# A longer clear between layer one's result scatters, and more results scattered before layer two's second sort

## The chip, the cores and the metric

One NeuronCore of a Trainium2 chip. The metric is the device time of one execution in microseconds, in float32 throughout. The profile names the engines PE (TensorE matmul; PEld its weight load), DVE (VectorE), ACT (ScalarE), POOL (GpSimd) and SP (SyncE, which issues most DMAs). POOL issues the indirect ones.

## The reference

The input x is 4 batches of 1024 tokens, width 128. Three sublayers follow one another, each a residual: a mixture of experts, an attention, the same mixture of experts again.

```python
x = x + 0.5 * ffn(layernorm(x))      # layer one
x = x + attn(layernorm(x))           # linear attention, 16 heads of 8, chunks of 128
x = x + 0.5 * ffn(layernorm(x))      # layer two, same weights

# ffn: each token goes to one of 8 experts (128 -> 512 -> 128)
expert_idx = argmax(xf @ Wr.T + br)
h = relu(xf @ W1[e].T + b1[e]);  y = h @ W2[e].T + b2[e]     # e = expert_idx of the token
```

## The kernel before, in words

**Sorting by expert.** Tokens lie in SBUF in 32 tiles of 128 rows. An expert layer works on tiles whose 128 tokens all have the same expert, so the rows are first sorted: for each token tile DVE computes where its rows go (`slot_of`, L792), and POOL writes the rows to DRAM with one indirect DMA per tile (`sort_rows`, L375 to L387). The sorted tiles are called slots here. A layer is sorted in two units, so that the first can be worked on while the second is still being routed. Layer one's units have 12 and 20 token tiles (19 and 27 slots), layer two's 16 and 16 (23 and 23 slots): 46 slots in each layer, 92 in all, numbered G = 0 to 91.

**One slot.** SP loads the slot's 128 rows of 576 bytes into a ring of 24 (`load_slot`, L309) and its expert's first weights, 256 KB, into a ring of four (`load_w1`, L318). DVE normalises (L818) and adds the second bias (L826), PE transposes (L1053), ACT copies (L509), PE multiplies up (L1061, 8 matmuls), ACT (L524) and DVE (L833) apply bias and relu, PE multiplies down (L1071, 8 matmuls), and DVE adds the result to the row in the ring (`add_y`, L840), which raises `y_done`. In the text "result n" is the n-th L840, of slot G = n - 1. Engines are tied by semaphores: PE signals the transpose, each half of up, and down to ACT, DVE and SP.

**Scatter.** POOL waits for `y_done`, clears a scratch tile that nothing reads (`pause`, L368, the MEMSET of L372) and sends the 128 rows back to their tokens' places with an indirect DMA (`scatter`, L389 to L399), to x1 in layer one and to the output in layer two. So a clear does nothing but put time between two indirect DMAs.

```python
for G in range(first, end):
    pool.wait_ge(y_done, G + 1)
    if G >= SCATTER_SEMS:
        wait_scattered(pool, G - SCATTER_SEMS)
    pause(256)
    pool.indirect_dma_start(...)
```

**Order on POOL** (L468 to L479), written by hand and kept in order by the engine:

```python
sort_rows(0); sort_rows(1)                  # sort_rows(1) has pause(512) before each DMA
scatter(0, LAYER_TILES - LATE)              # G = 0..37
for b in range(BATCH): outer_part(0, 1, b)
scatter(LAYER_TILES - LATE, LAYER_TILES - 6)  # G = 38, 39
for n in range(STEPS): attention(n)         # turn 0 holds G = 40..45, one by one
sort_rows(2)
scatter(LAYER_TILES, LAYER_TILES + EARLY_SCATTERS)
sort_rows(3)
scatter(LAYER_TILES + EARLY_SCATTERS, LAYERS * LAYER_TILES)
```

`sort_rows(0)`, `(2)` and `(3)` have no clear between their DMAs. Layer two's second sort, `sort_rows(3)`, waits for `slot_of` of that unit, which DVE computes beside slots 11 to 14 of the layer (the hooks of L1003 and L1004).

**Order on SP.** `loads` (L331) issues, in loop step G, the slot load of G + 6 and then the weight load of G + 3. The weight load waits until PE is done with slot G - 1's up product. The first slot load of a unit (G = 69 for the last one) waits for all of that unit's sort DMAs, and everything behind it on SP waits too, the weight load of G = 66 first. After all of layer one's scatters SP loads x1 back (L349), in attention's turn 0, for the layer norms of turn 1.

Of the kernel before, what the change touches and what calls it, by code (L numbers as in the profile page):

```python
# [83 lines left out]
def wait(eng, sem, value):  # L84
    if value > 0:
        eng.wait_ge(sem, value)
# [15 lines left out]
def build(nc, x, w1t, bias, w2t, wrt, br, wqkv, wg1t, wg2, wo, gamma, beta, decay, const, out):  # L102
    with ExitStack() as ctx:
# [147 lines left out]

        helped = lambda n, h: n < STEPS - 1 and h % 2 == 0
        ln_turn = lambda k: max(k + 1, 0)
        EARLY_SCATTERS = 6
        LATE = 8
        ROUTE_TURN = SPLIT[1][0] - 1 + 3

# [7 lines left out]
        layer_of = lambda G: G // LAYER_TILES  # L265
# [93 lines left out]
        def _(pool):  # L359
# [8 lines left out]
            def pause(columns):  # L368

                k = pauses[0]  # L370
                wait(pool, paused, k - 1)
                pool.memset(scratch[k % 2][:, 0:columns], 0.0).then_inc(paused, 1)  # L372
                pauses[0] += 1

            def sort_rows(u):  # L375
                unit = UNIT[u]
                pool.wait_ge(rows_kept, unit.layer * STEPS + (unit.first + unit.tiles) // BATCH)
                pool.wait_ge(fill_ready, 4)
                pool.wait_ge(ids_ready, 1 + 2 * min(u + 1, GROUPS))
                pool.wait_ge(slots_known[u], 1)  # L380
                pool.wait_ge(slots_filled[u], 16)
                for t in range(unit.tiles):
                    if u == 1:
                        pause(512)
                    pool.indirect_dma_start(  # L385
                        slots_in[u], bass.IndirectOffsetOnAxis(ap=slot_of[u][:, t:t + 1], axis=0),
                        row_of(unit.first + t), None).then_inc(rows_sorted[u], 16)  # L387

            def scatter(first, end):  # L389

                for G in range(first, end):
                    pool.wait_ge(y_done, G + 1)
                    if G >= SCATTER_SEMS:
                        wait_scattered(pool, G - SCATTER_SEMS)
                    pause(256)
                    pool.indirect_dma_start(  # L396
                        x1 if layer_of(G) == 0 else out, bass.IndirectOffsetOnAxis(ap=ids_in_ring(G), axis=0),
                        in_ring(G, 0, D), None, bounds_check=NO_TOKEN - 1,
                        oob_is_err=False).then_inc(scattered[G % SCATTER_SEMS], 16)  # L399
# [36 lines left out]
            def attention(n):  # L436

                late = lambda i: scatter(LAYER_TILES - 6 + i, LAYER_TILES - 5 + i) if n == 0 else None
                if n > 0:
                    outer_part(n, 1, 0)  # L440
# [27 lines left out]
            sort_rows(0)  # L468
            sort_rows(1)
            scatter(0, LAYER_TILES - LATE)  # L470
            for b in range(BATCH):
                outer_part(0, 1, b)
            scatter(LAYER_TILES - LATE, LAYER_TILES - 6)
            for n in range(STEPS):
                attention(n)
# [5 lines that stand above are left out]
# [821 lines left out]
```

## Time and profile before

| what | us |
|---|---|
| three runs before | 501.15, 503.57, 504.87 |
| their median | 503.57 |
| the profiled execution, whole | 504.27 |
| its span, first to last instruction | 502.5 |
| PE busy in the span | 376.0 |
| DVE busy | 347.6 |
| POOL busy | 301.8 |
| ACT busy | 192.8 |

The profile page shows shares over the whole span. Here the parts matter more: layer one's expert pass lies at about 46 to 170 us of the span, attention at 170 to 355, layer two's expert pass at 350 to 497. "remote" or "another core or an unknown queue" in a row is a wait that no event in the profile explains at the time when it ends. "issue" is idle time for which nothing was waited for that the profile shows.

### The profile page before, as it was taken

The page shows a single profiled execution, that of the slowest core. Times are in us where ns is not written, and L with a number is a line of the kernel's source. Part 1 is how long each engine was busy: PE and PEld are TensorE (multiplying, and loading weights), DVE is VectorE, ACT ScalarE, POOL GpSimd, SP SyncE. Part 2 cuts the span into 40 slices and gives each one's busy share as a digit, 9 for nine tenths or more (in the row PEclk, how much of TensorE's full clock was granted, in tenths as well). Part 3 has the DMA queues.
Part 4 walks back from the last instruction along what each step waited for, and adds up shares of the span by engine and source line. Part 5 has one row for each costly group of instructions (what it writes and reads, how often), then busy time and mean ns, then how long its engine had stood idle before and what let it go on. Part 6 is the DMA issues. An engine that isn't in the chain of part 4 may idle for free.

```text
span 502.5 us, 10537 instructions
## 1 busy us (share of the span) xinstructions
PE 376.0 (75%) x2474; PEld 331.9 (66%) x2474; DVE 347.6 (69%) x1064; ACT 192.8 (38%) x590; POOL 301.8 (60%) x386
## 2 busy tenths in 40 slices
PE   5693796699999859586797988372899720699983
PEld 2592796599988746465676776262798610699983
DVE  4937473178876796999989879994776700377861
ACT  1360452145546322336355352401565200255541
POOL 1047988856651796877847676765050378466564
PEclk9555798589999997999988979695699965699998
DMA  8982774257681008500000000012544321266630
GB/s 246 283 310 81 219 222 149 80 149 206 200 250 53 16 12 231 146 0 0 2 1 1 1 2 0 0 48 65 167 144 139 118 80 49 83 188 195 203 122 6
DMA packets 54218, 56.08 MB, mean 112 GB/s; under 512 B 6828, under 2 KB 39881, under 8 KB 53904
## 3 DMA queue, kind: packets, MB, share of 16 engines
q1 hardware_dynamic: 48736, 45.85, 31.8%
q0 software_dynamic: 4992, 8.94, 5.0%
q10 hardware_dynamic: 432, 0.63, 0.4%
q8 instruction: 23, 0.38, 0.3%
q14 instruction: 35, 0.29, 0.2%
HBM read 39.69 MB, written 17.53 MB: 114 GB/s over the span
## 4 chain that ended last, share of the span: by engine, by line
PE 26%; issue 25%; DVE 19%; POOL 15%; SPq 5%; another core or an unknown queue 4%; DMA 1%; ACT 1%; DVEq 1%; POOLq 1%; ACTq 0%
PE bank L1061 9%; PE bank L1071 9%; POOL out_x L396 7%; POOL scratch L372 3%; POOL slots_in L385 3%; DVE o_in L879 3%; PE bank L1153 2%; DVE st L666 2%; DVE qS L870 2%; PE bank L1119 2%; SPq L288 1%; PE bank L1025 1%; SPq L298 1%; POOL x L396 1%
## 5 line engine op out<-in xcount | busy, mean ns | idle before, releaser
L1061 PE MATMUL bank<-slot_xT,w_ring 128*128 128x128 f32 x736 | 110.0, 293 | 19.0 <-issue 8.6
L1061 PEld LDWEIGHTS bank<-slot_xT,w_ring 128*128 128x128 f32 x736 | 98.7, 206 | 23.8 <-issue 18.1
L385 POOL DMA_INDIRECT slots_in<-rows,slot_of x64 | 62.0, 969 | 67.1 <-DVE slot_of L792 51.3
L833 DVE TENSOR_SCALAR hT_b<-bank,b_cur 128x128 f32<-128x128 f32 x184 | 55.7, 344 | 40.3 <-remote 24.9
L1071 PE MATMUL bank<-w_sb,hT_a 128*128 x368 | 62.0, 293 | 23.1 <-issue 18.4
L1119 PE MATMUL bank<-outer_all,decay_sb 128*128 128x256 f32 x256 | 71.2, 405 | 10.4 <-POOL outer_all L277 6.8
L277 POOL TENSOR_TENSOR outer_all<-qkv 128x512 f32<-128x512 f32 x60 | 63.3, 1084 | 12.6 <-ACT qkv L562 12.5
L524 ACT ACTIVATE hT_a<-bank,b_cur 128x128 f32<-128x128 f32 x184 | 57.5, 364 | 31.5 <-remote 15.3
L1071 PEld LDWEIGHTS bank<-w_sb,hT_a 128*128 128x128 f32 x368 | 50.8, 200 | 27.7 <-issue 27.5
L1119 PEld LDWEIGHTS bank<-outer_all,decay_sb 128*128 128x128 f32 x256 | 49.4, 203 | 27.7 <-issue 8.1
L372 POOL MEMSET scratch<- 128x256 f32 (+1 forms) x112 | 40.3, 360 | 42.7 <-DVE ring L840 33.6
L840 DVE SCALAR_TENSOR_TENSOR ring<-bank,ring 128x128 f32<-128x128 f32 x92 | 26.6, 289 | 47.4 <-remote 21.0
L1071 PE MATMUL bank<-w_sb,hT_b 128*128 x368 | 58.5, 283 | 0.0
L396 POOL DMA_INDIRECT out_x<-ring x46 | 44.8, 974 | 19.0 <-POOL scratch L372 14.4
L879 DVE TENSOR_REDUCE o_in<-qS 128x64 f32<-128x256 f32 (+1 forms) x64 | 53.6, 858 | 0.0
L396 POOL DMA_INDIRECT x<-ring x46 | 45.4, 986 | 13.5 <-POOL scratch L372 10.5
L870 DVE TENSOR_TENSOR qS<-bank,qkv 128x512 f32<-128x512 f32 x64 | 43.3, 679 | 12.2 <-PE bank L1119 8.7
L1071 PEld LDWEIGHTS bank<-w_sb,hT_b 128*128 128x128 f32 x368 | 50.9, 200 | 0.0
L517 ACT ACTIVATE b_cur<-b_t 128x4 f32 x92 | 18.9, 205 | 69.9 <-DVE hT_b L833 48.3
L818 DVE TENSOR_SCALAR slot_n<-ring 128x128 f32<-128x128 f32 x92 | 44.0, 479 | 0.8 <-DMA ring<-slots_in 0.6
L434 POOL TENSOR_TENSOR qS<-qS 128x256 f32<-128x256 f32 x28 | 20.4, 729 | 39.3 <-DVE qS L870 39.2
L509 ACT ACTIVATE slot_xT<-bank 128x128 f32<-128x128 f32 x92 | 25.1, 273 | 46.8 <-remote 35.2
(119 smaller groups left out, 562.3 us busy)
## 6 DMA issues: line engine op xcount, KB each, us to landing
w_ring<-in_w1t SPq DMA_DIRECT2D x92, 256.0 KB
ring<-slots_in SPq DMA_DIRECT2D x92, 72.0 KB
slots_in<-fill SPq DMA_DIRECT2D x2, 1656.0 KB, 13.0
rows<-in_x SPq DMA_DIRECT2D x8, 256.0 KB, 6.2
w_sb<-in_w2t SPq DMA_DIRECT2D x1, 2048.0 KB
rows<-x SPq DMA_DIRECT2D x8, 256.0 KB, 4.9
slots_in<-fill SPq DMA_DIRECT2D x1, 1944.0 KB, 15.1
slots_in<-fill SPq DMA_DIRECT2D x1, 1368.0 KB, 8.7
```

The lines of the kernel that those rows point to most:

```text
L277: return eng.tensor_tensor(u_.rearrange("p (h d e) -> p h d e", d=HD, e=HD), k_.rearrange("p (h d) e -> p h d e", d=HD), v_, ALU.mult)
L372: pool.memset(scratch[k % 2][:, 0:columns], 0.0).then_inc(paused, 1)
L385: pool.indirect_dma_start(slots_in[u], bass.IndirectOffsetOnAxis(ap=slot_of[u][:, t:t + 1], axis=0), row_of(unit.first + t), None).then_in ...
L396: pool.indirect_dma_start(x1 if layer_of(G) == 0 else out, bass.IndirectOffsetOnAxis(ap=ids_in_ring(G), axis=0), in_ring(G, 0, D), None, b ...
L524: last = nc.scalar.activation(hT_a[G % 2][:, f * P:(f + 1) * P], bank_a[:, f * P:(f + 1) * P], ACT.Relu, bias=b1_cur[G % 2][:, f:f + 1])
L818: nc.vector.tensor_scalar(slot_n[G % 3][:, :], in_ring(G, 0, D), in_ring(G, SCALE_AT, SCALE_AT + 1), in_ring(G, SHIFT_AT, SHIFT_AT + 1), A ...
L833: last = nc.vector.tensor_scalar(hT_b[G % 2][:, f * P:(f + 1) * P], bank_b[:, f * P:(f + 1) * P], b1_cur[G % 2][:, 2 + f:3 + f], 0.0, ALU. ...
L870: nc.vector.tensor_tensor(qS[h % 4][:, :].rearrange("p (b a e) -> p b a e", b=BATCH, e=HD), bank[h % 3][:, :].rearrange("p (b a e) -> p b ...
L879: nc.vector.tensor_reduce(o_in[:, h * w:(h + 1) * w].rearrange("p (a e) -> p a e", e=HD), qS[h % 4][:, :].rearrange("p (a d e) -> p a e d" ...
L1061: last = mm(to[:, f * P:(f + 1) * P], w1_ring[G % W1_BUFS][:, (2 * half + f) * P:(2 * half + f + 1) * P], slot_xT[G % 2][:, :], start=True ...
L1071: last = mm(y_bank[:, 0:D], h[:, f % 2 * P:(f % 2 + 1) * P], w2_sb[:, bass.ds(expert[G] + f * D, D)], start=(f == 0), stop=(f == FB - 1))
L1119: last = mm(to, decay_sb[:, (2 * h + a) * P:(2 * h + a + 1) * P], u, start=True, stop=True)
```

## The change

Between layer one's scatters POOL clears 128 x 512 elements, before 128 x 256. Layer two's stay at 256. And `EARLY_SCATTERS` is 15, before 6: POOL scatters G = 46 to 60 before `sort_rows(3)`, before it was G = 46 to 51.

```diff
--- before.py
+++ after.py
@@ -251,7 +251,7 @@
 
         helped = lambda n, h: n < STEPS - 1 and h % 2 == 0
         ln_turn = lambda k: max(k + 1, 0)
-        EARLY_SCATTERS = 6
+        EARLY_SCATTERS = 15
         LATE = 8
         ROUTE_TURN = SPLIT[1][0] - 1 + 3
 
@@ -392,7 +392,7 @@
                     pool.wait_ge(y_done, G + 1)
                     if G >= SCATTER_SEMS:
                         wait_scattered(pool, G - SCATTER_SEMS)
-                    pause(256)
+                    pause(512 if layer_of(G) == 0 else 256)
                     pool.indirect_dma_start(
                         x1 if layer_of(G) == 0 else out, bass.IndirectOffsetOnAxis(ap=ids_in_ring(G), axis=0),
                         in_ring(G, 0, D), None, bounds_check=NO_TOKEN - 1,
```

## Rows read from the trace of the kernel before

**Rows 1.** the page's part 4, the chain that ended last, by engine
```profile
PE 26%; issue 25%; DVE 19%; POOL 15%; SPq 5%; another core or an unknown queue 4%; DMA 1%; ACT 1%; DVEq 1%; POOLq 1%; ACTq 0%
```

**Rows 2.** windows: stretch, length, busy us by engine, PEclk, DMA share, GB/s
```profile
46.00:79.00 33.00, 27.89 (x238) 26.69 (x238) 20.62 (x70) 13.94 (x53) 29.70 (x40) 0.83 0.70 208
...
79.00:101.00 22.00, 13.50 (x64) 11.45 (x64) 5.22 (x18) 3.59 (x14) 18.40 (x29) 0.63 0.31 95
...
397.00:417.00 20.00, 6.81 (x38) 5.45 (x38) 4.24 (x18) 2.20 (x9) 15.42 (x16) 0.72 0.27 88
...
417.00:430.00 13.00, 1.81 (x8) 1.78 (x8) 0.84 (x3) 0.00 (x0) 11.52 (x19) 0.50 0.14 46
```

**Rows 3.** timeline of POOL, layer one: start us, length us, what, idle before
```profile
77.55 0.54 POOL L372 MEMSET scratch<- 128x512 f32 x1
...
79.22 0.33 POOL L372 MEMSET scratch<- 128x256 f32 x1
...
98.74 0.97 POOL L396 DMA_INDIRECT x<-ring  x1 [0.16 <-issue]
...
161.56 2.09 POOL L277 TENSOR_TENSOR outer_all<-qkv 128x512 f32<-128x512 f32 x2 [11.42 <-ACT qkv L562]
```

**Rows 4.** timeline of DVE, layer one: results 2, 11, 17 and 36
```profile
60.43 0.29 DVE L840 SCALAR_TENSOR_TENSOR ring<-bank,ring 128x128 f32<-128x128 f32 x1 [0.25 <-PE bank L1071]
...
78.03 0.29 DVE L840 SCALAR_TENSOR_TENSOR ring<-bank,ring 128x128 f32<-128x128 f32 x1
...
106.66 0.29 DVE L840 SCALAR_TENSOR_TENSOR ring<-bank,ring 128x128 f32<-128x128 f32 x1 [0.28 <-PE bank L1071]
...
142.93 0.28 DVE L840 SCALAR_TENSOR_TENSOR ring<-bank,ring 128x128 f32<-128x128 f32 x1
```

**Rows 5.** timeline of all engines behind the very first sort
```profile
48.20 0.48 PE L1053 MATMUL bank<-const_sb,slot_n 128*128 128x128 f32 x1 [0.23 <-issue]
...
52.99 0.28 ACT L509 ACTIVATE slot_xT<-bank 128x128 f32<-128x128 f32 x1 [8.29 <-remote]
```

**Rows 6.** line L818 in 46 to 79 and in 104 to 143: ns min/median/max
```profile
L818 DVE TENSOR_SCALAR slot_n<-ring x15: 335/375/803, 47.8 to 78.2; 128x128 f32<-128x128 f32 x15
...
L818 DVE TENSOR_SCALAR slot_n<-ring x20: 535/535/656, 104.4 to 141.2; 128x128 f32<-128x128 f32 x20
```

**Rows 7.** timeline of attention's turn 0, last scatter and what follows
```profile
187.45 1.02 POOL L396 DMA_INDIRECT x<-ring  x1 [0.17 <-issue]
...
189.67 2.59 SPq L327 DMA_DIRECT2D rows<-x  x5
```

**Rows 8.** timeline of POOL around the last sort
```profile
397.00 0.96 POOL L385 DMA_INDIRECT slots_in<-rows,slot_of  x1 [18.55 <-DVE slot_of L792]
...
416.07 0.95 POOL L385 DMA_INDIRECT slots_in<-rows,slot_of  x1 [0.30 <-issue]
...
429.24 0.97 POOL L396 DMA_INDIRECT out_x<-ring  x1 [0.17 <-issue]
```

**Rows 9.** timeline, other engines around the last sort: results 60, 61, 63, 67 are L840
```profile
400.30 0.27 DVE L840 SCALAR_TENSOR_TENSOR ring<-bank,ring 128x128 f32<-128x128 f32 x1
...
401.86 0.61 PE L1071 MATMUL bank<-w_sb,hT_b 128*128 x4
...
418.37 0.32 SPq L316 DMA_DIRECT2D ring<-slots_in  x1
...
427.62 0.29 DVE L840 SCALAR_TENSOR_TENSOR ring<-bank,ring 128x128 f32<-128x128 f32 x1 [15.64 <-remote]
...
436.91 0.29 DVE L840 SCALAR_TENSOR_TENSOR ring<-bank,ring 128x128 f32<-128x128 f32 x1 [0.74 <-PE bank L1071]
...
444.65 0.29 DVE L840 SCALAR_TENSOR_TENSOR ring<-bank,ring 128x128 f32<-128x128 f32 x1 [0.30 <-PE bank L1071]
```

**Rows 10.** timeline around layer two's first sort, in attention
```profile
347.10 0.96 POOL L385 DMA_INDIRECT slots_in<-rows,slot_of  x1 [0.30 <-issue]
...
350.93 0.69 DVE L889 TENSOR_TENSOR o_all<-bank,o_in 128x512 f32<-128x512 f32 x1 [2.70 <-remote]
```

## Prediction

> **What bounds the kernel now.** I read the chain that ended last first, then the busy shares in stretches, then the timelines of the two stretches that stood out. The chain [rows 1] names no single engine: a quarter is PE, a quarter "issue", and 4% is "another core or an unknown queue", although there is one core. The stretches show where that lies [rows 2]. From 46 to 79 us PE works 27.89 of 33 us at a granted clock of 0.83. From 79 to 101 it works 13.50 of 22 us at 0.63, from 397 to 417 6.81 of 20, and from 417 to 430 1.81 of 13 us at 0.50, which is its lower level of 1.2 GHz. In the last three the DMA engines are used at 0.14 to 0.31, less than the 0.70 of the stretch that runs well, so they aren't full.
>
> Common to the bad stretches is that POOL issues indirect DMAs close together. The last sort does 16 from 397.00 to 417.02, one each 1.27 us; nine scatters then end at 430.21 [rows 8]. PE had finished the down product of slot 60 at 402.47, but DVE takes it up only at 427.62, with 15.64 us of "remote" before it [rows 9]. So it is PE's signals to the others that arrive late, and the engines wait for one another. How close the DMAs stand decides. In layer one the second sort clears 512 columns, and a step of POOL takes 1.67 us (77.55 to 79.22); then come 14 scatters with 256 columns, in (99.71 - 79.22)/14 = 1.46 us each [rows 3]. Results come at (78.03 - 60.43)/9 = 1.956 us during the former, but the six from 78.03 to 106.66 take 28.63 us [rows 4]. From there POOL has caught up and works in step with PE; results come at (142.93 - 106.66)/19 = 1.909 us [rows 4]. A late signal also recovers under the 512 clear: right behind the first, unspaced sort the transpose that ended at 48.68 was taken up at 52.99 [rows 5], and then there is no such wait before 79.
>
> **Part 1, 512 columns in layer one.** It adds one thing 46 times: a clear takes 0.54 instead of 0.33 us, 0.21 more [rows 3]. A backlogged scatter then takes 1.67 us like a sort DMA, as their indirect DMAs are equally long, 0.97 [rows 3, 8].
> - The gain: six results in 6 x 1.956 = 11.7 us instead of 28.63 [rows 4], 16.9 us. That a scatter at 1.67 us leaves PE's signals alone is taken from the sort; no row shows such a scatter. The ends are +16.9 and a loss (second rival).
> - POOL falls behind less slowly: it starts 11 results behind at 79.22 and works at 1.67 against 1.956 us, so scatter 37 ends at 79.22 + 38 x 1.67 = 142.7. Its next work, the outer products, can start at 161.56 now [rows 3], about 146.6 then. 4 us of cover are left. If it were gone, attention would start later by what POOL lacks. The ring holds 24 slots and SP wants scatter G - 18, so a backlog of 11 doesn't stop it.
> - The clears now stand beside the 21 further results too: (1.956 - 1.909) x 21 = 1.0 us lost.
> - DVE's L818 takes 335 ns alone, 535 in the median beside a 256 clear, and 803 at most beside 512 [rows 6]. In the five slots at the end of the pass where DVE also has layer norm work, I count 0.2 each, 1.0 us (ends 0 and 5 x 0.47 = 2.3).
> - Eight scatters stand behind the outer products and in turn 0. The last one (187.45) frees SP's reload of x1 (189.67) [rows 7], which turn 1 needs. 8 x 0.21 = 1.7 at most, 0 at least; I take half, 0.9.
> Sum: 16.9 - 1.0 - 1.0 - 0.9 = 14.0 us gained. The ends are 16.9 and -4.4 (second rival).
>
> On DVE, the Trainium skill, SBUF — State Buffer, "Who interferes with whom", says that DVE and GpSimd hold a shared port pair by an exclusive lock, each for a whole instruction, and that only this contends. It speaks against this change: if DVE bounded every slot, 46 x 0.21 = 9.7 us would be lost. The lengthened L818 agrees with the lock [rows 6]; the 1.956 against 1.909 us say that PE's pace hides nearly all of it. The same section has no place for PE being held up by POOL, as [rows 2, 9] show it.
>
> **Part 2, 15 scatters before the last sort.** Nine scatters move from behind the sort to before it. They are issued as results come, in step with PE, so they need no wait of their own. But the sort, and on SP slot 69 and weight load 66 behind it, now wait for result 61.
> - Result 60 is at 400.30 and the down product for 61 ends at 402.47 [rows 9], so result 61 would be at 402.7 without the block. The nine clears stand beside DVE's routing; for the five slots where that routing makes DVE late I add 0.2 each, 1.0 us: 403.7. The last scatter takes 1.9 from there, and the sort starts at 405.6 instead of 397.00 and ends at 425.6.
> - Before, the sort began at about result 58.9; POOL came to rest at 430.21 and result 63 was there 6.7 us later, 436.91 [rows 8, 9]: 4.1 results from start to recovery.
> - After, it begins at result 62.0. The first few signals pass as before, so two or three results are waiting when it ends: three scatters of 1.46, POOL rests at 430.0, and result 66.1 is there at 436.7. Before, that was at 444.65 - 0.9 x 1.93 = 442.9 [rows 9]: 6.2 us. With two waiting it is 7.7. I take 7.
> - The upper end: if signals recover as soon as the sort ends, SP still passes slot 69 only 1.35 us after it (418.37 less 417.02) [rows 8, 9], at 427.0. I estimate that the weights of slot 66 take from their issue as long as the last scatter took to release SP, 2.2 us [rows 7]: 429.2. That slot's up product stands two slot times ahead of result 67, so it ran at about 444.65 - 2 x 1.93 = 440.8, and 11.6 us is the most. Layer two's first sort, with no scatters behind it, had signals back 2.9 us after its end (348.06 to 350.93) [rows 10], so this isn't far off.
> - The lower end: -2.6 (first rival).
>
> **Sum.** 14.0 + 7 = 21.0 us from the profiled execution's 504.27: 483.3. That execution is 0.7 above the median of the runs, so 482.6; I say 483.
>
> **The rivals.**
> 1. The block runs its 33.2 us from the sort's start (397.00 to 430.21), whatever stands behind it. Then result 66.1 comes at 405.6 + 33.2 + 6.7 = 445.5, 2.6 later than before, and only part 1 counts: 504.3 - 14.0 + 2.6 = 493. For it: the block did last through the scatters. Against: the recovery after layer two's first sort [rows 10].
> 2. Scatters at 1.67 us still block. POOL was 11 results behind and had caught up after 14 scatters, so PE gave three in those 20.5 us [rows 3], 0.146 per us. At 0.599 scatters per us instead of 0.683 the backlog is gone after 11/(0.599 - 0.146) = 24.3 us instead of 20.5. PE makes 0.6 of a result in the 3.8 us more, so 2.7 are lost, with the clears of turn 0 3.6 to 4.4. With part 2: 504.3 + 3.6 - 7 = 501. Against: the 512 phase that ran clean, and recovered [rows 4, 5].
> 3. The other side. It is the number of indirect DMAs that blocks, not the gaps. Then both places lose: 4.4 in layer one and 2.6 at the last sort: 504.3 + 7.0 = 511. It decides from the point where one DMA each 1.67 us blocks like one each 1.46. In step at 1.9 us nothing blocks, so that point would have to lie between.
> 4. Signals come back as soon as the last sort ends. 504.3 - 14.0 - 11.6 = 478.7, and with part 1 free of its small losses 476.
>
> The Trainium skill, DMA: Bandwidth & Descriptors, "Issuing engines are not separate DMA queues", says that DMAs of all engines share the same 16 DMA engines and interleave. By it, crowded DMA engines would be the cause, spacing would matter only for the traffic, and the first rival's 493 or worse would be the time. The DMA share of 0.14 to 0.31 in the bad stretches [rows 2] is against it.
>
> **How the numbers follow.** Forecast 0.60, first rival 0.13, second 0.10, third 0.05, fourth 0.12. A measurement of this kernel can tell about 1% from no change, that is 498.5 to 508.6. Faster: 0.60 + 0.13 + 0.12 = 0.85; within: 0.10; slower: 0.05. The range goes from below the fourth rival's 476 to beyond the first's 493: 474 to 496.
>
> **What would show it.** Part 1 is right if the stretch 79 to 101 has PE busy as in 46 to 79 with a granted clock near 1, no "remote" waits, result 17 near 90 us instead of 106.66, and POOL's scatters back to back until about 143. Part 2 is right if the last sort starts some 8 us later against its surroundings, and fewer than four scatters stand back to back behind it. Wrong would be "remote" waits of DVE and ACT in 79 to 101, or nine results' worth of idle PE still behind the sort, or POOL late for the outer products.

## The result, and the profile after

| what | before, us | after, us |
|---|---|---|
| median of the timed runs, one chip | 504.22 (4 runs) | 484.0 (4 runs) |
| lowest to highest | 501.15 to 506.77 | 478.16 to 486.81 |
| the profiled execution, whole | 504.27 | 483.07 |
| its span | 502.5 | 481.3 |
| PE, DVE, POOL busy | 376.0, 347.6, 301.8 | 368.5, 346.9, 312.2 |

The ratio is 0.956, with a 95% interval of [0.945, 0.967]. The ratios in this document compare only runs in the chip's faster state (of the four after the change all but 486.81), so they aren't the quotients of the medians beside them. 483.0 was forecast. A second set on another chip gave 483.95 (6 runs) against 502.56 (11 runs), 0.962 [0.959, 0.966].

The windows of the changed kernel, first the two stretches of [rows 2] in layer one, then the last sort, which stands elsewhere now:

```profile
46.00:79.00 33.00, 27.84 (x237) 26.68 (x238) 20.44 (x69) 13.63 (x52) 29.70 (x40) 0.82 0.72 208
79.00:101.00 22.00, 21.96 (x187) 21.11 (x187) 15.93 (x55) 11.30 (x43) 19.85 (x27) 1.00 0.67 199
385.00:400.00 15.00, 9.41 (x64) 8.24 (x64) 5.11 (x18) 3.59 (x14) 10.74 (x13) 0.85 0.22 73
400.00:420.00 20.00, 6.74 (x31) 6.18 (x32) 3.57 (x12) 2.73 (x10) 12.38 (x16) 0.52 0.32 97
```

The second line is part 1's success: PE is busy in 21.96 of 22 us at a granted clock of 1.00, where it was 13.50 at 0.63. The last line shows that the stall at the last sort is still there; it has become shorter, not gone.

The chain that ended last, by engine, against [rows 1]:

```profile
issue 26%; PE 25%; POOL 21%; DVE 20%; DMA 2%; another core or an unknown queue 2%; POOLq 1%; DVEq 1%; ACT 0%; ACTq 0%; SPq 0%
```

The unknown part went from 4% to 2%. POOL's share rose from 15% to 21%; its steps are longer, which would do that, but a chain can also take another path.

The timeline of layer one, against [rows 3, 4]:

```profile
78.37 0.29 DVE L840 SCALAR_TENSOR_TENSOR ring<-bank,ring 128x128 f32<-128x128 f32 x1
...
88.77 0.98 POOL L396 DMA_INDIRECT x<-ring  x1 [0.16 <-POOL scratch L372]
...
90.27 0.29 DVE L840 SCALAR_TENSOR_TENSOR ring<-bank,ring 128x128 f32<-128x128 f32 x1
90.45 0.97 POOL L396 DMA_INDIRECT x<-ring  x1 [0.16 <-POOL scratch L372]
...
142.63 1.05 POOL L396 DMA_INDIRECT x<-ring  x1 [0.16 <-issue]
148.21 2.09 POOL L277 TENSOR_TENSOR outer_all<-qkv 128x512 f32<-128x512 f32 x2 [4.53 <-ACT qkv L562]
```

Results 11 and 17 are the two L840 rows, 11.90 us apart where it was 28.63. The scatters beside them stand 1.68 us apart. Scatter 37 ends at 143.68, and POOL still rests 4.53 us before the outer products, which wait for ACT.

The timeline around the last sort, against [rows 8, 9]:

```profile
388.91 0.29 DVE L840 SCALAR_TENSOR_TENSOR ring<-bank,ring 128x128 f32<-128x128 f32 x1 [0.25 <-PE bank L1071]
389.38 0.96 POOL L385 DMA_INDIRECT slots_in<-rows,slot_of  x1 [0.30 <-issue]
...
395.29 0.29 DVE L840 SCALAR_TENSOR_TENSOR ring<-bank,ring 128x128 f32<-128x128 f32 x1 [2.26 <-remote]
...
405.95 0.61 DVE L833 TENSOR_SCALAR hT_b<-bank,b_cur 128x128 f32<-128x128 f32 x2 [9.53 <-remote]
...
408.36 0.96 POOL L385 DMA_INDIRECT slots_in<-rows,slot_of  x1 [0.30 <-issue]
...
409.81 0.98 POOL L396 DMA_INDIRECT out_x<-ring  x1 [0.16 <-POOL scratch L372]
...
411.29 0.98 POOL L396 DMA_INDIRECT out_x<-ring  x1 [0.16 <-issue]
...
415.14 0.29 DVE L840 SCALAR_TENSOR_TENSOR ring<-bank,ring 128x128 f32<-128x128 f32 x1 [8.58 <-remote]
...
415.49 0.31 POOL L372 MEMSET scratch<- 128x256 f32 x1 [3.22 <-DVE ring L840]
```

The L840 rows are results 62, 63 and 64. Two scatters stand in a row behind the sort, where there were nine. POOL rests at 412.27, and 2.87 us later (415.14) the signals are back, as after layer two's first sort [rows 10]. The waits of "remote" inside the sort, 9.53 us here, are as before.

Where the time went, by the moment at which the same thing happens in both profiled executions:

| moment | before | after | gained so far |
|---|---|---|---|
| result 11 | 78.03 | 78.37 | -0.3 |
| result 17 | 106.66 | 90.27 | 16.4 |
| result 38 | 148.10 | 134.58 | 13.5 |
| result 46, end of the pass | 169.82 | 156.46 | 13.4 |
| last scatter of layer one | 187.45 | 174.96 | 12.5 |
| result 47, start of layer two's pass | 363.13 | 348.17 | 15.0 |
| result 67, behind the last sort | 444.65 | 422.41 | 22.2 |
| result 92 | 495.04 | 473.84 | 21.2 |

### The profile page after: what moved, and what is told of

Same layout as the page of the kernel before. It is cut to its first block, busy times and chain, and to the rows that moved or that the text cites. A ratio compares the mean times of both kernels' runs of the same rounds, so it can differ in the third digit from the quotient of the medians.

```text
span 481.3 us, 10537 instructions
## 1 busy us (share of the span) xinstructions
PE 368.5 (77%) x2474; PEld 323.9 (67%) x2474; DVE 346.9 (72%) x1064; ACT 191.3 (40%) x590; POOL 312.2 (65%) x386
## 4 chain that ended last, share of the span: by engine, by line
issue 26%; PE 25%; POOL 21%; DVE 20%; DMA 2%; another core or an unknown queue 2%; POOLq 1%; DVEq 1%; ACT 0%; ACTq 0%; SPq 0%
POOL out_x L396 9%; PE bank L1071 8%; PE bank L1061 7%; POOL slots_in L385 6%; POOL scratch L372 4%; DVE o_in L879 4%; PE bank L1119 3%; DVE st L666 2%; PE bank L1031 2%; PE bank L1025 2%; PE bank L1099 2%; PE bank L1153 1%; POOL x L396 1%; DMA br_sb<-in_br 1%
## 5 line engine op out<-in xcount | busy, mean ns | idle before, releaser
L1061 PE MATMUL bank<-slot_xT,w_ring 128*128 128x128 f32 x736 | 106.3, 287 | 14.6 <-issue 8.8
L1061 PEld LDWEIGHTS bank<-slot_xT,w_ring 128*128 128x128 f32 x736 | 95.6, 201 | 18.5 <-issue 12.6
L372 POOL MEMSET scratch<- 128x512 f32 (+1 forms) x112 | 50.3, 449 | 43.9 <-DVE ring L840 38.9
L1119 PE MATMUL bank<-outer_all,decay_sb 128*128 128x256 f32 x256 | 70.2, 400 | 11.1 <-POOL outer_all L277 8.0
L840 DVE SCALAR_TENSOR_TENSOR ring<-bank,ring 128x128 f32<-128x128 f32 x92 | 26.7, 290 | 37.1 <-PE bank L1071 14.2
L818 DVE TENSOR_SCALAR slot_n<-ring 128x128 f32<-128x128 f32 x92 | 42.7, 465 | 0.8 <-DMA ring<-slots_in 0.6
L826 DVE TENSOR_TENSOR ring<-ring,b_sb 128x128 f32<-128x128 f32 x92 | 27.0, 294 | 19.2 <-issue 12.5
## 6 DMA issues: line engine op xcount, KB each, us to landing
slots_in<-fill SPq DMA_DIRECT2D x2, 1656.0 KB, 12.9
slots_in<-fill SPq DMA_DIRECT2D x1, 1944.0 KB, 14.9
```

Source lines behind the costliest of these rows:

```text
L818: nc.vector.tensor_scalar(slot_n[G % 3][:, :], in_ring(G, 0, D), in_ring(G, SCALE_AT, SCALE_AT + 1), in_ring(G, SHIFT_AT, SHIFT_AT + 1), A ...
L1061: last = mm(to[:, f * P:(f + 1) * P], w1_ring[G % W1_BUFS][:, (2 * half + f) * P:(2 * half + f + 1) * P], slot_xT[G % 2][:, :], start=True ...
L1119: last = mm(to, decay_sb[:, (2 * h + a) * P:(2 * h + a + 1) * P], u, start=True, stop=True)
```

## The experiments

The theory: what holds up PE's signals is the gap between POOL's indirect DMAs. At 1.67 us from one to the next a running stream of signals stays nearly whole; at 1.46 and 1.27 us it doesn't, and a block lasts until POOL has had a rest. The rivals: the number of such DMAs, the traffic or memory port of the clears themselves, and a block of fixed length from the sort's start. The kernels below were run in three batches, each on one chip with the kernel before beside them: 500.53 us (492.79 to 503.14, 13 runs), 503.88 (499.02 to 507.47, 7 runs) and 502.56 (499.48 to 504.63, 11 runs). As these medians differ and a stage differs from one execution to another, I read the mechanism from distances between results within a profiled execution, one for each kernel: 11 to 17 (the backlog behind layer one's second sort), 11 to 46 (the pass from there), and 47 to 67 (layer two's pass over the last sort). The table is at the end of this section.

Each diff stands against the changed kernel, where nothing else is said.

**Each part alone.** e1_part1:

```diff
-        EARLY_SCATTERS = 15
+        EARLY_SCATTERS = 6
```

> Only part 1: clears of 512 columns in layer one, EARLY_SCATTERS back at 6. If the two parts act independently, layer one runs as in the changed kernel (result 17 near 90 us, result 46 near 156) and the last sort as in the kernel before: 40 us from its start to the fourth result behind it, with nine scatters in a row behind it. Time: the changed kernel's 484.0 plus the 7.3 us that results 47 to 67 gained = 491. Rival (the block is counted from the sort's start, so that part 2 gives nothing): 484.

e2_part2:

```diff
-                    pause(512 if layer_of(G) == 0 else 256)
+                    pause(256)
```

> Only part 2: EARLY_SCATTERS 15, clears of 256 columns everywhere in the scatters. Layer one runs as before: result 17 near 106.7, with waits for PE's signals from 79 to 101. The last sort runs as in the changed kernel: two or three scatters in a row behind it. Time: before 504.2 less 7 = 497. Rival (part 2 gives nothing): 504.

e1_part1 took 491.08 us (486.57 to 491.33, 4 runs), ratio 0.986 [0.965, 1.006]; e2_part2 491.24 (489.76 to 497.13, 10 runs), 0.992 [0.984, 0.999]. The intervals are too wide to split the gain between the parts. The distances do: with part 1 alone results 11 to 46 take 75.85 us (before 91.79) and 47 to 67 take 80.99 (before 81.52); with part 2 alone it is 89.11 and 74.73. So each part works in its own stretch and leaves the other's alone, and by the distances each is worth alone about what it is worth in the changed kernel, 13.7 to 15.9 us and 6 to 7 us. The same layer-one code gives 91.79 us in one execution and 89.11 in another, so some 2.7 us of such a difference can be the execution's. The whole times show less: by their ratios 7 us for part 1 and 4 for part 2, against 19 to 22 for both together. The intervals reach to 17 and 8 us, so this doesn't contradict the distances, but it doesn't confirm them either. The kernel before was not profiled on that chip. In e2_part2 the 256 clear in layer one still shows the block:

```profile
84.22 0.29 DVE L840 SCALAR_TENSOR_TENSOR ring<-bank,ring 128x128 f32<-128x128 f32 x1 [2.41 <-remote]
...
90.92 0.28 ACT L509 ACTIVATE slot_xT<-bank 128x128 f32<-128x128 f32 x1 [2.06 <-remote]
```

**A step between: 384 columns in layer one.**

```diff
-                    pause(512 if layer_of(G) == 0 else 256)
+                    pause(384 if layer_of(G) == 0 else 256)
```

> The changed kernel with clears of 384 instead of 512 columns in layer one: one scatter each 1.57 us, between the 1.46 that blocked and the 1.67 that did not. If the block grows gradually as the gaps shrink, result 17 falls between 90.3 and 106.7, near 95, and the time is near 488. If there is a threshold below 1.57, result 17 is at 90 as with 512, and the later results come a little closer together than the 2.07 us seen with 512: 483. If it is above, 106 and 500.

489.33 us (487.08 to 490.46, 4 runs), 0.986 [0.969, 1.004]. Timeline behind the second sort:

```profile
85.62 0.97 POOL L396 DMA_INDIRECT x<-ring  x1 [0.17 <-POOL scratch L372]
...
87.19 0.97 POOL L396 DMA_INDIRECT x<-ring  x1 [0.17 <-POOL scratch L372]
...
88.63 0.62 ACT L524 ACTIVATE hT_a<-bank,b_cur 128x128 f32<-128x128 f32 x2 [1.21 <-remote]
...
90.23 0.29 DVE L840 SCALAR_TENSOR_TENSOR ring<-bank,ring 128x128 f32<-128x128 f32 x1 [0.93 <-PE bank L1071]
...
91.74 0.62 ACT L524 ACTIVATE hT_a<-bank,b_cur 128x128 f32<-128x128 f32 x2 [1.20 <-remote]
...
93.34 0.29 DVE L840 SCALAR_TENSOR_TENSOR ring<-bank,ring 128x128 f32<-128x128 f32 x1 [0.93 <-PE bank L1071]
```

At 1.57 us from scatter to scatter the first half of up reaches ACT some 1.2 us late and the down product reaches DVE 0.9 us late, and a result takes 3.11 us (90.23 to 93.34). Results 11 to 17 take 16.54 us, the 19 behind them 41.76, and 11 to 46 takes 85.04, between 91.79 and some 76.5. So it isn't a switch between 1.46 and 1.67 us: lateness falls as the gap grows.

**Is it the clear or the gap?** e6_one_partition keeps the length of each clear, but it writes one partition, not 128:

```diff
-                pool.memset(scratch[k % 2][:, 0:columns], 0.0).then_inc(paused, 1)
+                pool.memset(scratch[k % 2][0:1, 0:columns], 0.0).then_inc(paused, 1)
```

> The changed kernel with clears of the same length on one partition instead of 128. If only the time between two indirect DMAs counts, everything stays: 1.67 us per scatter, results 11 to 17 in 12 us, and the same from result 47 to 67. If it is the clear's own writes over all partitions that matter (slowing DVE's L818, or making way for PE's signals in another manner), results 17 to 36 come at 1.91 instead of 2.0 us, or the late signals return.

488.74 us, one run. Some 4.3 us of this arise before the pass gets going (result 1 at 62.99, in the changed kernel 58.66). Then:

```profile
80.47 0.52 POOL L372 MEMSET scratch<- 1x512 f32 x1
81.16 0.98 POOL L396 DMA_INDIRECT x<-ring  x1 [0.17 <-issue]
...
82.82 0.97 POOL L396 DMA_INDIRECT x<-ring  x1 [0.17 <-POOL scratch L372]
```

A scatter every 1.66 us here (1.65 in the median), written data 128 times smaller, and results 11 to 17 take 12.43 us, 47 to 67 74.55: the two gains stay. For them the clear is worth its length alone, not what it writes. The clears as such can't be what blocks: the last sort has none and is the worst stretch. The 19 results from 17 take 41.25 us, 1.9 more than in the changed kernel. Its steps are 1.65 us in the median instead of 1.67, and ACT and DVE take up PE's signals there up to 0.9 us late, in the changed kernel up to 0.6. Such a small step in the gap would act this way by the theory, but one execution doesn't show it.

**Spacing the last sort too.** e4_sort_spaced is the changed kernel with `pause(512)` before each DMA of `sort_rows(3)`, as `sort_rows(1)` has it:

```diff
-                    if u == 1:
+                    if u in (1, 3):
```

> The changed kernel with a clear of 512 columns before each DMA of layer two's second sort too. The pace theory expects no late signals of PE there any more: no remote waits of ACT and DVE of over 2 us around that sort, results 63 to 65 about 1.9 us apart. But the sort takes 16 x 1.67 = 26.7 instead of 20.2 us, and SP issues the weights of slot 66 only behind it, so that PE then waits for weights and the time stays within 2 us of the changed kernel. The rival (the number of indirect DMAs blocks, not their pace) expects the remote waits to stay and some 6 us more than the changed kernel.

482.45 us, one run. In 345 to 440 us there is no wait of "remote" at all. The sort now takes 26.05 us instead of 19.94, and results 61 to 65 come beside it at 1.9 us each. Then PE stops:

```profile
411.77 0.96 POOL L385 DMA_INDIRECT slots_in<-rows,slot_of  x1 [0.17 <-POOL scratch L372]
...
414.08 0.32 SPq L316 DMA_DIRECT2D ring<-slots_in  x1
415.14 0.34 SPq L324 DMA_DIRECT2D w_ring<-in_w1t  x1
...
418.18 2.04 PE L1061 MATMUL bank<-slot_xT,w_ring 128*128 128x128 f32 x8 [26.59 <-issue]
```

Slot 69's load waits on SP for the whole sort, slot 66's weights are queued behind it and are issued at 415.14, and the up product for slot 66 (result 67 is its) starts at 418.18. So the block is gone and the SP queue has taken its place: 47 to 67 takes 78.25 us, 4.0 more than in the changed kernel. It is a stall cured and a stall exposed.

**Start the spaced sort earlier.** e5_12_spaced takes `EARLY_SCATTERS` 12, the spaced sort, and 512 columns between layer two's scatters as well:

```diff
-        EARLY_SCATTERS = 15
+        EARLY_SCATTERS = 12
-                    if u == 1:
+                    if u in (1, 3):
-                    pause(512 if layer_of(G) == 0 else 256)
+                    pause(512)
```

> EARLY_SCATTERS 12, clears of 512 columns before the DMAs of the last sort and before every scatter of both layers. With 12 the sort no longer waits for a result: slot_of is ready about then. It starts some 8 us sooner than with 15 and, spaced, lasts 26 us; no late signals of PE. PE then waits for the weights of slot 66, 5.5 us behind the sort's end as with 15. From result 47 to 67 it takes 70 us instead of the changed kernel's 74.2 and the spaced 15's 78.3. POOL has 34 scatters at 1.67 us left, 57 us, about as long as PE has work. Time 2 to 4 us under the changed kernel on the same chip. Rival: POOL becomes the bound of the end, and the time is the changed kernel's or more.

480.94 us (480.05 to 483.96, 4 runs), 0.957 [0.949, 0.965]. 47 to 67 takes 71.53, 6.7 less than in e4_sort_spaced. The weights still come late:

```profile
414.27 0.34 SPq L324 DMA_DIRECT2D w_ring<-in_w1t  x1
...
417.33 2.05 PE L1061 MATMUL bank<-slot_xT,w_ring 128*128 128x128 f32 x8 [18.38 <-issue]
```

**Fewer slots ahead on SP.** e8_slots4 is e5_12_spaced with slot loads four slots ahead instead of six, so that slot 69's load stands behind the weights of slot 67, not in front of those of slot 66 (diff against e5_12_spaced):

```diff
-            SLOTS_AHEAD, W1_AHEAD, X1_AT = 6, 3, 34
+            SLOTS_AHEAD, W1_AHEAD, X1_AT = 4, 3, 34
```

> As EARLY_SCATTERS 12 with everything spaced at 512, and SP loads slots 4 ahead instead of 6, so that the weights of slots 66 and 67 are issued before SP waits for the last sort. If the wait for those weights bounds PE there, PE works on two slots more during the sort and results 47 to 67 take 3 to 4 us less than with 6 ahead. Rival: the shorter lead lets slot loads arrive late everywhere, and both layers' results come further apart than 2.0 us.

479.30 us (475.18 to 483.60, 4 runs), 0.949 [0.937, 0.960]. Windows of it around the sort:

```profile
385.00:400.00 15.00, 13.12 (x111) 12.37 (x110) 11.39 (x44) 6.41 (x25) 12.96 (x18) 1.00 0.47 148
400.00:420.00 20.00, 5.53 (x41) 5.07 (x40) 3.96 (x13) 2.53 (x11) 18.02 (x24) 0.70 0.25 78
```

PE is busy in 13.12 of 15 us beside the spaced sort and then runs out of work, as the rows of slot 69 and, behind them on SP, the weights of slot 68 come only when the sort is done. Result 67 comes 65.22 us behind 47, but 68 another 4.2 later, so 68 is the fair mark: 69.42 against 73.42 in e5_12_spaced. The shorter lead costs nothing that shows in layer one (11 to 46: 78.37 against 78.09).

**Does 1.67 us lift a block that stands?** e7_6_l2_spaced leaves the last sort unspaced and `EARLY_SCATTERS` at 6, so nine scatters stand in a row behind it, now at 1.68 us each:

```diff
-        EARLY_SCATTERS = 15
+        EARLY_SCATTERS = 6
-                    pause(512 if layer_of(G) == 0 else 256)
+                    pause(512)
```

> EARLY_SCATTERS 6 with clears of 512 columns in layer two's scatters as well. What part 2 removed is either nine scatters close together behind the sort (then spacing them does the same: the third result behind the sort's end comes some 10 us after it instead of 19, and results 47 to 67 take 74 instead of 81 us), or it is PE's head start before the sort (then they still take 81). The longer backlog may cost 1 to 2 us at the end.

485.46 us (485.42 and 485.50), 0.964 [0.955, 0.974]. 47 to 67 takes 81.81 us, no better than before's 81.52. The sort ends at 399.92:

```profile
400.63 0.99 POOL L396 DMA_INDIRECT out_x<-ring  x1 [0.16 <-issue]
...
407.04 0.29 DVE L840 SCALAR_TENSOR_TENSOR ring<-bank,ring 128x128 f32<-128x128 f32 x1 [12.82 <-remote]
...
408.49 0.28 ACT L509 ACTIVATE slot_xT<-bank 128x128 f32<-128x128 f32 x1 [13.95 <-remote]
...
414.06 0.97 POOL L396 DMA_INDIRECT out_x<-ring  x1 [0.17 <-issue]
...
418.51 0.29 DVE L840 SCALAR_TENSOR_TENSOR ring<-bank,ring 128x128 f32<-128x128 f32 x1 [1.02 <-PE bank L1071]
```

Result 63 (418.51) comes 18.6 us behind the sort's end; I had expected some 10, as [rows 5], a recovery beside 512 clears, pointed that way. It is the run that corrects the picture most: a gap of 1.68 us doesn't make new lateness, but it hardly works off what has piled up.

**Nine scatters behind the sort, but a rest first.** e9_rest is the same kernel with one wait between the sort and the scatters. No scatter is taken away or moved:

```diff
             sort_rows(3)
+            pool.wait_ge(y_done, LAYER_TILES + 16)
             scatter(LAYER_TILES + EARLY_SCATTERS, LAYERS * LAYER_TILES)
```

> EARLY_SCATTERS 6 and clears of 512 columns in layer two's scatters, as in the run before it, and one wait more: behind the last sort POOL rests until result 62 is there. If the signals come back only when POOL rests (2.9 us after an unspaced sort), result 61 comes some 3 us after the sort's end and result 63 some 8 us after it instead of 18.6, and results 47 to 67 take about 72 instead of 81.8 us. Then what part 2 removed was the row of scatters behind the sort. If it was PE's head start, result 63 still comes 18 us after the sort's end and the 81.8 us stay.

478.23 us, one run. The diff stands against e7_6_l2_spaced. The sort ends at 400.03, 0.1 us from where it did there:

```profile
400.56 0.29 DVE L841 SCALAR_TENSOR_TENSOR ring<-bank,ring 128x128 f32<-128x128 f32 x1 [7.82 <-remote]
...
402.69 0.28 ACT L510 ACTIVATE slot_xT<-bank 128x128 f32<-128x128 f32 x1 [9.62 <-remote]
...
403.35 0.28 DVE L841 SCALAR_TENSOR_TENSOR ring<-bank,ring 128x128 f32<-128x128 f32 x1
403.69 0.53 POOL L372 MEMSET scratch<- 128x512 f32 x1 [3.67 <-DVE ring L841]
404.45 0.99 POOL L396 DMA_INDIRECT out_x<-ring  x1 [0.23 <-POOL scratch L372]
...
407.42 0.29 DVE L841 SCALAR_TENSOR_TENSOR ring<-bank,ring 128x128 f32<-128x128 f32 x1 [1.10 <-PE bank L1072]
```

(The added line makes L840 into L841.) Result 62 is there 3.3 us behind the sort's end, result 63 7.4 us behind it instead of 18.6. 47 to 67 takes 68.88 us, 12.9 less than in e7_6_l2_spaced and also less than the 74.24 of the changed kernel, whose sort starts later. I had expected about 72. One edit tells it: the row of DMAs standing directly behind the sort is what stretches the block, and with POOL at rest it is over within 3 us. The same nine scatters at 1.68 us behind the rest make no signal late. The whole execution gains less than the stretch, 7.2 us against e7_6_l2_spaced (on another chip), because POOL has become the bound of the end: after the rest it works at 1.68 us per scatter without a pause, and its last scatter starts at 470.09, 6.5 us behind result 92 (463.59). In every other kernel here that distance is 1.1 us.

**Between 384 and 512.** e10_448 is e8_slots4 with 448 columns between layer two's scatters (diff against that):

```diff
-                    pause(512)
+                    pause(512 if layer_of(G) == 0 else 448)
```

> As the next-to-last one, with clears of 448 instead of 512 columns between layer two's scatters: 1.62 us each. If POOL's 34 scatters bound the end, results 67 to 92 take 1.5 to 2 us less. If signals come late again at 1.62 us, they take as long or longer.

477.10 us (473.63 to 480.46, 4 runs), 0.948 [0.942, 0.953]. With a scatter every 1.62 us, results 68 to 92 take 48.92 us where e8_slots4 has 47.32. POOL's shorter step should have saved up to 2 us and cost 1.6 instead. Single signals are again late there, by 0.3 to 0.9 us and once by 1.2. So in this execution trimming the gap gained nothing; the whole times (477.10 against 473.56 for b1_best on the same chip, with ranges that overlap) don't separate the two.

**The changed kernel and the best one on one chip.** a2_changed is the kernel after the change, b1_best is e8_slots4 once more.

> The changed kernel as it is, once more, beside the next one on the same chip: about 4% under the kernel before, and 2 to 5 us over the next one.

> EARLY_SCATTERS 12, every scatter and the last sort spaced at 512 columns, slots loaded 4 ahead, once more with more rounds: results 47 to 67 in 65 us and 67 to 92 in 51.5 us as in its first run, so the changed kernel's 125.7 us from result 47 to 92 become 117, less what attention varies by, and POOL's last scatter is what ends the run.

a2_changed took 483.95 us (479.98 to 484.57, 6 runs), b1_best 473.56 (470.56 to 478.73, 6 runs), 0.942 [0.937, 0.947]. That is 10.4 us below the changed kernel on the same chip, where 2 to 5 had been expected. It beats both kernels, and no other of this study has a lower median.

The distances in us between results, from the profiled executions:

| kernel | 11 to 17 | 11 to 46 | 47 to 67 | 47 to 80 | 68 to 92 |
|---|---|---|---|---|---|
| before | 28.63 | 91.79 | 81.52 | 106.91 | 48.50 |
| after | 11.90 | 78.09 | 74.24 | 99.19 | 49.53 |
| a2_changed | 11.50 | 76.07 | 75.72 | 100.66 | 47.76 |
| e1_part1 | 11.75 | 75.85 | 80.99 | 105.94 | 47.72 |
| e2_part2 | 26.07 | 89.11 | 74.73 | 99.68 | 47.93 |
| e3_384 | 16.54 | 85.04 | 74.35 | 99.31 | 47.70 |
| e4_sort_spaced | 11.45 | 75.46 | 78.25 | 103.20 | 47.69 |
| e5_12_spaced | 11.89 | 78.09 | 71.53 | 96.80 | 46.37 |
| e6_one_partition | 12.43 | 80.08 | 74.55 | 99.50 | 49.45 |
| e7_6_l2_spaced | 11.93 | 76.68 | 81.81 | 107.20 | 46.69 |
| e8_slots4 | 11.89 | 78.37 | 65.22 | 93.09 | 47.32 |
| b1_best | 11.80 | 76.54 | 64.99 | 93.29 | 47.16 |
| e9_rest | 11.88 | 75.36 | 68.88 | 94.15 | 46.43 |
| e10_448 | 11.96 | 76.48 | 64.83 | 95.13 | 48.92 |

## Why the prediction was right, and where not

The time (483.0 against 484.0) and both mechanisms held; the parts of the sum, by its own steps:

- **Results 11 to 17, 16.9 us.** Measured 16.7 (28.63 to 11.90), and 11.45 to 11.96 us in the other kernels with full 512 clears in layer one. The one thing that no row had shown, that a scatter at 1.67 us leaves PE's signals alone like a sort DMA, was right. The second and third rival needed the opposite.
- **POOL's backlog** until 142.7, outer products at 146.6: 143.68 and 148.21. The cover held and was 4.5 us instead of 4.
- **1.0 us for the clears beside 21 more results.** Results 17 to 38 take 44.31 us instead of 41.44, 2.9 lost. The term was mis-sized, for two reasons. The step I extrapolated from held a clear in step with PE; here the backlog lasts until result 38, so the gap is 1.68, and there a few signals are a little late. A down product (97.62 for 0.61 us) ends at 98.23 and is taken up at 98.65, a transpose (98.07 for 0.27) ends at 98.34 and is taken up at 98.68:

```profile
98.65 0.29 DVE L840 SCALAR_TENSOR_TENSOR ring<-bank,ring 128x128 f32<-128x128 f32 x1 [0.63 <-PE bank L1071]
98.68 0.28 ACT L509 ACTIVATE slot_xT<-bank 128x128 f32<-128x128 f32 x1 [0.34 <-PE bank L1053]
```

  And it differs by execution: the 19 results from 17 to 36 take 36.27 us before, 39.34 here, and 36.98 to 38.95 in the other kernels with the same code in layer one. So the loss is 0.7 to 3.1 us, and 1.0 is at its lower end. Added up over results 17 to 38, the idle times of ACT and DVE of 0.15 us and more in front of a late signal of PE are 6.0 us here, 0.2 to 5.8 in the others with this code, and 13.5 in e6_one_partition; the three executions with this code that need 44.0 to 44.5 us for these results (the changed kernel's, e5_12_spaced, e8_slots4) have 4.2 to 6.0 us of it, those that need 41.7 to 42.9 have 0.2 to 4.5. The other ground that the prediction named, DVE's L818 growing beside longer clears, isn't it: it became shorter in the median, as fewer of the clears fall beside it (compare [rows 6]):

```profile
L818 DVE TENSOR_SCALAR slot_n<-ring x18: 335/340/685, 105.1 to 142.5; 128x128 f32<-128x128 f32 x18
```

- **1.0 us on DVE at the end of the pass.** Results 38 to 46 take 21.88 instead of 21.72, 0.2 lost. The cover holds: DVE's own longer L818 doesn't reach PE. The Trainium skill, SBUF — State Buffer, "Who interferes with whom", describes the exclusive port lock that I had weighed for this. The trace agrees that it is there: in layer one of the changed kernel each of the 16 L818 of over 450 ns overlaps a clear. So do the 16 in e6_one_partition, up to 744 ns: clears of one partition don't take the lock away, and that run is no test of what it costs. The 0.2 us are what shows here.
- **0.9 us for the eight clears in turn 0.** Measured 0.9: the lead shrinks from 13.4 us at result 46 to 12.5 at the last scatter.
- Sum of part 1: 14.0 forecast, 12.5 in the profiled execution. From result 11 to 46 the forecast was 91.79 - 14.9 = 76.9; the changed kernel has 78.09, a2_changed 76.07.
- **Attention** had no term. It gained 2.5 us from the last scatter of layer one to result 47. That needn't be the change's: results 46 to 47 take 193.3 us before, 191.7 after, 193.8 in a2_changed, and from 188.9 to 196.4 over all the kernels, with single turns 1 to 2.5 us longer in different places. I can't explain that scatter between executions.
- **Part 2, 7 us (6.2 to 7.7).** Measured 7.3 from result 47 to 67 (5.8 in a2_changed, 6.8 in e2_part2). The sort starts 7.3 us later against result 47, forecast 8.6. Two scatters stand behind it, forecast two or three. The first rival, a block of fixed length, is out by e9_rest, in which it ends with the sort. The fourth, that it ends with the sort by itself whatever stands behind it, is out by e7_6_l2_spaced.
- **The last 25 results.** 67 to 92 take 51.43 instead of 50.39, 1.0 us lost, not forecast. It need not be the change's: a2_changed takes 49.66. A timeline of the changed kernel shows late signals on a small scale here too:

```profile
453.82 0.97 POOL L396 DMA_INDIRECT out_x<-ring  x1 [1.98 <-issue]
...
455.27 0.97 POOL L396 DMA_INDIRECT out_x<-ring  x1 [0.16 <-issue]
...
456.73 0.97 POOL L396 DMA_INDIRECT out_x<-ring  x1 [0.16 <-issue]
...
458.16 0.63 ACT L524 ACTIVATE hT_a<-bank,b_cur 128x128 f32<-128x128 f32 x2 [2.69 <-remote]
```

  Three scatters fall together at 1.46 us, and a signal to ACT is 2.69 us late. This stall stands in before too, with 1.95 us, so it isn't what the 1.0 us are. With 512 columns in layer two as well, results 68 to 92 take 46.37 to 47.32 us; with 256 it is 47.69 to 49.53.

So 21.0 was forecast and 21.2 came: -1.5 in part 1, +0.3 in part 2, +2.5 in attention and -1.0 at the end. The closeness is partly luck, as two terms without a forecast (+2.5 and -1.0) stand in it; what held is the two large ones.

The Trainium skill, DMA: Bandwidth & Descriptors, "Issuing engines are not separate DMA queues", says that DMAs of all engines run on the same 16 DMA engines. The reading of that rule came out as weighed. In the changed kernel the stretch 79 to 101 moves twice the data per us (0.67 instead of 0.31 DMA share), and no signal in it is over 0.6 us late, so crowded DMA engines aren't the cause.

## What to carry to other kernels

When several engines idle together and the profile names no releaser, look for what a third engine does in steady rhythm at that time, not for a resource that is full: here the DMA engines were used least where it was worst. Where POOL issues indirect DMAs beside a PE pipeline, give each a filler of some tenths of a us until the step is about 1.7 us, and never let a row of others follow directly behind an unspaced burst; a wait of 3.7 us behind the burst, on a result that was coming anyway, gave 12.9 us back in that stretch (e9_rest against e7_6_l2_spaced), of which 7.2 were left at the end, as POOL ran out of slack. And when a stall is cured, ask which queue it had been hiding: here the SP queue with the next weights behind the sort's own load, which cost the spaced sort 4.0 us in its stretch. An earlier sort brought it below the changed kernel (71.53 against 74.24 us), and a shorter slot lead brought the rest.

## What the runs showed of the hardware that was not expected

- PE's signals to ACT and DVE are late by an amount that falls with the distance of POOL's indirect DMAs. By the idle time in front of the engine that takes them up: around the sort at 1.27 us per DMA up to 15.6 us for the down product [rows 9] (25.2 us from PE's end, 402.47, to 427.62), at 1.46 1.2 to 3.4, at 1.57 up to 1.2 in most slots, at 1.62 to 1.68 mostly none or a few tenths (up to 1.2 at 1.62, 0.9 at 1.65), and in step at 1.9 us not to be seen. The number of DMAs (e9_rest), the clear's width (e6_one_partition) and the DMA share don't decide.
- Signals in the other direction weren't held up where they can be followed. In the worst stretch of the kernel before, DVE ends result 61 at 427.91 and PE goes on at 428.19, and ACT ends at 407.71 and PE at 407.85:

```profile
407.08 0.63 ACT L524 ACTIVATE hT_a<-bank,b_cur 128x128 f32<-128x128 f32 x2 [5.51 <-remote]
...
407.85 1.19 PE L1061 MATMUL bank<-slot_xT,w_ring 128*128 128x128 f32 x4 [5.27 <-ACT hT_a L524]
```

  As the profile models the ends of matmuls, it can't tell a signal that is late from a product that really ends late.
- Lateness piles up and is a debt. A row at 1.68 us leaves it standing for some 15 us (e7_6_l2_spaced). With POOL at rest it is gone in 2.9 us (changed kernel) or 0.5 to 2.7 (e9_rest: 400.56 and 402.69 against the sort's end at 400.03).
- This looks like something that serves POOL's indirect DMAs and PE's signals in one line, with some 1.5 us for each DMA of 128 rows. That figure is an estimate from the gaps at which lateness grows and doesn't: at 1.46 us (kernel before) the time from PE's end to the uptake goes from 1.7 us (80.20 to 81.94) to 6.2 (94.32 to 100.52), at 1.57 (e3_384) it stays at about 1.0 to 1.7. The mechanism is a hypothesis: no run looked into it. Whether fewer rows per DMA would need a smaller gap wasn't tried.
